# Latent attention: values of two key tiles in one place, rough pieces between the heads of a score step, 24 pieces ahead of a pair of heads

## What is computed

```python
c_q = _rmsnorm(x @ Wq_down, q_norm_w)
q = (c_q @ Wq_up).reshape(b, s, H, HD).transpose(0, 2, 1, 3)
...
c_kv = _rmsnorm(x @ Wkv_down, kv_norm_w)
k = (c_kv @ Wk_up).reshape(b, s, H, HD).transpose(0, 2, 1, 3)
...
scores = (jnp.einsum('bhqd,bhkd->bhqk', q, k) + jnp.einsum('bhqd,bhkd->bhqk', q_rope, k_rope)) * scale
attn = jax.nn.softmax(scores, axis=-1)
out = jnp.einsum('bhqk,bhkd->bhqd', attn, v)
```

## Time and profile before

| | us |
|---|---|
| median of 3 runs | 2254.46 |
| the runs | 2253.89 to 2258.62 |
| the profiled execution | 2254.67 |
| its span, from the first to the last instruction | 2252.9 |
| a pair in the middle of a sequence | 61.3 |

### The profile page before, as it was taken

One profiled execution on the slowest core, in us unless ns is written; L12 is line 12 of the kernel. 1 busy time (PEld: TensorE's weight loads), 2 busy tenths in 40 slices (PEclk: granted clock), 3 DMA queues, 4 the chain that ended last, 5 costly groups with the idle time before them and its releaser, 6 DMA issues. The chain is left out here.

```text
span 2252.9 us, 29291 instructions
## 1 busy us (share of the span) xinstructions
PE 2004.6 (89%) x8700; PEld 1245.8 (55%) x8701; DVE 1301.1 (58%) x2970; ACT 785.7 (35%) x1293; POOL 866.8 (38%) x684
## 2 busy tenths in 40 slices
PE   5899868889888799967599999999899999999987
PEld 5566635545554666646455555555565555555456
DVE  7322275777785722237466666666656666666525
ACT  1122244555555122223223333333413333433323
POOL 0344301231112044432026555556425555565632
PEclk9999969999999599988579999999999999999999
DMA  9111132331220811132331122122122222211101
GB/s 380 47 63 58 54 122 29 42 44 29 29 29 7 341 56 60 61 103 109 73 69 42 46 56 50 38 54 56 22 63 57 57 52 56 56 45 42 31 0 50
DMA packets 60569, 150.62 MB, mean 67 GB/s; under 512 B 12977, under 2 KB 18305, under 8 KB 58177
## 3 DMA queue, kind: packets, MB, share of 16 engines
q1 hardware_dynamic: 50208, 120.43, 20.4%
q0 software_dynamic: 9120, 24.92, 3.5%
q10 hardware_dynamic: 1152, 4.19, 0.5%
HBM read 68.95 MB, written 18.61 MB: 39 GB/s over the span
## 5 line engine op out<-in xcount | busy, mean ns | idle before, releaser
L1831 POOL TENSOR_TENSOR mla_PS<-mla_PS,mla_PT 128x1024 f32<-128x1024 f32 x192 | 457.7, 2384 | 222.2 <-ACT mla_PT L2110 219.6
L2253 DVE TENSOR_REDUCE mla_MXP<-PS 128x1 f32<-128x512 f32 x512 | 343.3, 689 | 241.9 <-PE PS L1910 236.6
L2110 ACT ACTIVATE mla_PT<-PS 128x1024 f32<-128x1024 f32 x256 | 262.4, 1026 | 401.9 <-PE PS L1929 399.5
L1938 PE MATMUL PS<-mla_PT,mla_CN 128*64 128x512 f32 x1024 | 275.3, 616 | 0.1
L1910 PE MATMUL PS<-mla_KH,mla_QH 113*128 113x512 f32 x512 | 216.6, 459 | 30.1 <-DMA mla_KL<-mla_SL 18.8
L521 DVE COPY moe_HT<-PS 128x512 f32<-128x512 f32 x92 | 63.6, 692 | 306.9 <-PE PS L644 301.0
L1929 PE MATMUL PS<-mla_QH,mla_KH 113*128 113x512 f32 x512 | 211.3, 413 | 1.0 <-ACT mla_QH L2097 1.0
L675 POOL DMA_INDIRECT moe_XS<-rows_in,moe_GI x96 | 93.5, 974 | 307.1 <-PE PS L630 171.7
L1929 PE MATMUL PS<-mla_QL,mla_KH 113*128 113x512 f32 x512 | 202.2, 395 | 0.0
L1929 PE MATMUL PS<-mla_QH,mla_KL 113*128 113x512 f32 x512 | 201.3, 393 | 0.0
L1910 PEld LDWEIGHTS PS<-mla_KH,mla_QH 113*128 113x128 f32 x512 | 90.7, 193 | 192.0 <-DVE mla_MXP L2253 123.5
(11 more groups left out here) (297 smaller groups left out, 3203.2 us busy)
## 6 DMA issues: line engine op xcount, KB each, us to landing
W<-in_W_dram SPq DMA_DIRECT2D x16, 2048.0 KB, 28.1
mla_QH<-mla_SH SPq DMA_DIRECT2D x64, 128.0 KB, 2.4
mla_KH<-mla_SH SPq DMA_DIRECT2D x64, 128.0 KB, 2.4
mla_QL<-mla_SL SPq DMA_DIRECT2D x64, 128.0 KB, 2.5
mla_KL<-mla_SL SPq DMA_DIRECT2D x64, 128.0 KB, 2.4
mla_KH<-mla_SH SPq DMA_DIRECT2D x64, 96.0 KB, 2.4
mla_KL<-mla_SL SPq DMA_DIRECT2D x64, 96.0 KB, 2.4
sums_Y<-rows_out SPq DMA_DIRECT2D x9, 512.0 KB, 6.1
```

The lines of the kernel that those rows point to most:

```text
L1831: pool.tensor_tensor(PS[:, :], PT[:, slot(0), :] if k == 1 else PS[:, :], PT[:, slot(k), :], ALU.add).then_inc(s_ps.handle, 1)
L1938: ins = pe.matmul(bank(6)[h * DKVL:(h + 1) * DKVL, :], CN[:, b, k, 0:DKVL], PT[:, slot(k), h * HB:(h + 1) * HB], start=(k == 0), stop=(k = ...
L2110: act.activation(PT[:, slot(k), :], banks(st_bank(s, 0), 2)[:, :], ACT.Exp, scale=MLA_SCALE).then_inc(s_p.handle, 1)
L2253: dve.tensor_reduce(MXP[:, n // NPC, c, h, t:t + 1], bank(piece_bank(n))[:, :], AX_X, ALU.max).then_inc(s_mx.handle, 1)
```

## The change

The values of step m are no longer computed in step m + 1, each in a place of its own. The table `WITH` puts those of two steps together: at step 0 those of the last two steps of the pair before, at 2, 4 and 6 those of steps 0 to 5, at 7 and 8 one each (steps 6 and 7, the end of a query block), at 10, 12 and 14 those of steps 8 to 13. Steps 1, 3, 5, 9, 11, 13 and 15 have none. `PT`'s three slots now go round (`SLOT`), and `exp_of` waits for what `in_slot_until` names. The first rough piece of a step moves between the two heads of `scores_of`, except at steps 2 and 9. In the second half of a pair the second piece stands ahead of the values. `LATE` sums to 24 instead of 22, `EARLY` to 8 instead of 10. ACT's `out_copy` of the block before moves behind the first exponential of a pair.

```diff
-    LATE, EARLY = {9: 3, 10: 3, 11: 3, 12: 3, 13: 4, 14: 3, 15: 3}, {2: 1, 3: 2, 4: 3, 5: 2, 6: 2}
+    LATE, EARLY = {9: 2, 10: 4, 11: 3, 12: 4, 13: 3, 14: 5, 15: 3}, {2: 2, 3: 1, 4: 2, 5: 1, 6: 2}
...
-    slot = lambda k: 2 if k == 0 else k % 2
+    WITH = {0: (-2, -1), 2: (0, 1), 4: (2, 3), 6: (4, 5), 7: (6,), 8: (7,), 10: (8, 9), 12: (10, 11), 14: (12, 13)}
+    SLOT = (0, 1, 2, 0, 1, 2, 0, 1, 2, 0, 1, 2, 0, 1, 2, 1)
+    in_slot_until = lambda s: max(p for p in range(-NS, s) if SLOT[p % NS] == SLOT[s])
...
                             for n, (kk, qq) in enumerate(((KH, QH), (KH, QL), (KL, QH))):
                                 ins = pe.matmul(bank(st_bank(s, h))[:, :], kk[USED, buf, h, ks], qq[USED, buf, h, qs], start=(n == 0), stop=(n == 2))
+                            if h == 0:
+                                rough_scores(*near, between)
                         ins.then_inc(s_st.handle, 1)
...
-                            scores_of(it, buf, s, first and s < 2)
+                            between = 0 if s in (2, 9) else 1
+                            scores_of(it, buf, s, first and s < 2, near, todo[:between])
...
-                            if s == 8:
-                                denominators(2 * it)
-                            rough_scores(*near, todo[:1])
-                            if s == 0 and not first:
-                                denominators(2 * it - 1)
...
+                            rough_scores(*near, todo[between:1 if s < TB else 2])
+                            if s == 8:
+                                denominators(2 * it)
+                            if s == 0 and not first:
+                                denominators(2 * it - 1)
                             if s or not first:
-                                values_of(NS * it + s - 1, 2 * it + (s - 1) // TB, (s - 1) % TB)
-                            rough_scores(*near, todo[1:2])
+                                for m in WITH.get(s, ()):
+                                    values_of(NS * it + m, 2 * it + m // TB, m % TB, m % NS)
...
-                            rough_scores(*near, todo[2:])
+                            rough_scores(*near, todo[1 if s < TB else 2:])
...
                         if last:
-                            values_of(NS * it + NS - 1, 2 * it + 1, TB - 1)
+                            for m in (NS - 2, NS - 1):
+                                values_of(NS * it + m, 2 * it + m // TB, m % TB, m % NS)
...
-                        if not free:
-                            if k == 0:
-                                act.wait_ge(s_ps.handle, s_ps.at((TB - 1) * (blk - 1) + 1))
-                                act.wait_ge(s_v.handle, s_v.at(TB * (blk - 1) + 1))
-                            else:
-                                act.wait_ge(s_v.handle, s_v.at(NS * it + s - 1))
-                                act.wait_ge(s_ps.handle, s_ps.at((TB - 1) * blk + (k - 2 if k > 2 else k - 3 + 2 * (k == 1))))
+                        p = in_slot_until(s)
+                        if p >= 0 or not free:
+                            act.wait_ge(s_v.handle, s_v.at(NS * it + p + 1))
+                            act.wait_ge(s_ps.handle, s_ps.at((TB - 1) * (2 * it + p // TB) + max(p % TB, 1)))
```

More of the change, by code:

```diff
@@ L1830, in sums @@
                                 pool.wait_ge(s_ps.handle, s_ps.at((TB - 1) * blk + k - 1))
-                            pool.tensor_tensor(PS[:, :], PT[:, slot(0), :] if k == 1 else PS[:, :], PT[:, slot(k), :], ALU.add).then_inc(s_ps.handle, 1)
+                            pool.tensor_tensor(PS[:, :], PT[:, SLOT[TB * q], :] if k == 1 else PS[:, :], PT[:, SLOT[TB * q + k], :], ALU.add).then_inc(s_ps.handle, 1)
                     def pair(it, r, buf, first, last, after=None):
@@ L1918, in max_rows, with scores_of @@
                         ins.then_inc(s_mt.handle, 1)
-                    def scores_of(it, buf, s, free):
+                    def scores_of(it, buf, s, free, near, between):
                         q, k = s // TB, s % TB
@@ L1929, in scores_of, with values_of @@
                                 ins = pe.matmul(bank(st_bank(s, h))[:, :], kk[USED, buf, h, ks], qq[USED, buf, h, qs], start=(n == 0), stop=(n == 2))
+                            if h == 0:
+                                rough_scores(*near, between)
                         ins.then_inc(s_st.handle, 1)
-                    def values_of(step, blk, k):
+                    def values_of(step, blk, k, at):
                         pe.wait_ge(s_p.handle, s_p.at(step + 1))
@@ L1937, in values_of @@
                         for h in range(2):
-                            ins = pe.matmul(bank(6)[h * DKVL:(h + 1) * DKVL, :], CN[:, b, k, 0:DKVL], PT[:, slot(k), h * HB:(h + 1) * HB],
+                            ins = pe.matmul(bank(6)[h * DKVL:(h + 1) * DKVL, :], CN[:, b, k, 0:DKVL], PT[:, SLOT[at], h * HB:(h + 1) * HB],
                                             start=(k == 0), stop=(k == TB - 1))
@@ L2102, in exp_of @@
                         act.wait_ge(s_st.handle, s_st.at(NS * it + s + 1))
-                        if not free:
-                            if k == 0:
-                                act.wait_ge(s_ps.handle, s_ps.at((TB - 1) * (blk - 1) + 1))
-                                act.wait_ge(s_v.handle, s_v.at(TB * (blk - 1) + 1))
-                            else:
-                                act.wait_ge(s_v.handle, s_v.at(NS * it + s - 1))
-                                act.wait_ge(s_ps.handle, s_ps.at((TB - 1) * blk + (k - 2 if k > 2 else k - 3 + 2 * (k == 1))))
-                        act.activation(PT[:, slot(k), :], banks(st_bank(s, 0), 2)[:, :], ACT.Exp, scale=MLA_SCALE).then_inc(s_p.handle, 1)
+                        p = in_slot_until(s)
+                        if p >= 0 or not free:
+                            act.wait_ge(s_v.handle, s_v.at(NS * it + p + 1))
+                            act.wait_ge(s_ps.handle, s_ps.at((TB - 1) * (2 * it + p // TB) + max(p % TB, 1)))
+                        act.activation(PT[:, SLOT[s], :], banks(st_bank(s, 0), 2)[:, :], ACT.Exp, scale=MLA_SCALE).then_inc(s_p.handle, 1)
                     def out_copy(blk):
@@ L2118, in pair @@
                         for s in range(NS):
-                            if s == 0 and not first:
-                                out_copy(2 * it - 1)
                             if not last:
@@ L2129, in pair @@
                                     weights_high(it + 2, r + 2)
-                            exp_of(it, s, first and s < 3)
+                            exp_of(it, s, first)
+                            if s == 0 and not first:
+                                out_copy(2 * it - 1)
                             if not last:
```

## The result

| | before | after |
|---|---|---|
| median, us | 2254.89 (8 runs) | 2269.88 (8 runs) |
| the runs, us | 2251.04 to 2258.62 | 2263.5 to 2275.38 |
| span of the profiled execution, us | 2252.9 | 2268.4 |
| a pair in the middle of a sequence, us | 61.4 | 62.3 |

The ratio is 1.0064, with a 95% interval of 1.0054 to 1.0075: 15 us, slower. The forecast was 2260, slower by 5, with a range of 2234 to 2273. The pair lengths here are distances between the joins of step 13, over six pairs (1742.1 to 2110.3 before, 1749.8 to 2123.9 after), which the moved exponential of step 0 does not disturb.

The account below looks back on a forecast made before the run. PE, busy 59.6 of a middle pair's 61.3 us, was taken as the bound. Terms summed to +0.44, taken as +0.55 a pair, +7.7 over 14 pairs; with the ends +5.4 on 2254.67 gave 2260 us, range 2234 to 2273.

Parts of the forecast that it names:

- values side by side, 7 places: Values in a middle pair go from 16 places to 9; each merging gives 0.35 us on PE: -2.45 a pair.
- `max_rows` at step 7: Join still ends with POOL's add, 4.15 us stays; PE waits 0.24 instead of 0.87 us: -0.63 a pair.
- `max_rows` at step 14: Join of step 13 asks 0.3 to 0.4 us behind the add's start and waits for its end: +1.82.
- the slow piece, from step 13 to step 14: Step 13's fourth piece cost 0.83 us, waiting for a maximum; the same wait comes behind step 14's values: 0.
- denominators at step 0: PE arrives at 3.54 us but POOL's last add lets it go at 4.14: +0.60 a pair.
- small waits of pieces: Pieces wait for bank A maxima at steps 2 to 5, +0.72, and behind `latent_out` at step 12, +0.4: +1.1.
- a price between the heads: Rival: nine pieces each followed at 0.34 instead of 0.23 us, with 0.05 wait; 1.4 a pair, 2280 us; chance 0.14.
- one of my own signs of being wrong: The forecast is wrong if distances behind pieces between the heads are mostly 0.34 us.
- The ends: Last pair about -2.4 us, last pair of the first sequence -1.2, two more pieces ahead of the first pair +1.3.
- At nothing: Two pieces more ahead of a pair are two fewer in it, put down at no cost.

Follow-up runs that it names:

- one input: The kernel after, with DVE's join of the maxima as a reduction over one SBUF input: 2240.22 us, ratio 0.9941. The same edit on the kernel before: 2256.56 us.
- half an add: The kernel after, with POOL adding only 512 of 1024 columns in adds behind a block's first, computing something else: 2242.9 us, ratio 0.9944.
- the run with the pieces of steps 3 and 5: The kernel after, with the piece of steps 3 and 5 behind the scores instead of between their heads: 2267.53 us, ratio 1.0065.
- the run with none between: The kernel after with the one-input join and all pieces behind the scores, none between the heads: 2247.64 us, ratio 0.9966.
- the runs with the tables: The kernel after with before's LATE and EARLY: 2295.12 us; with before's LATE and two early pieces in each of steps 2 to 6: 2281.72 us.

## Why the prediction came out as it did, by its own steps

The terms for a middle pair, forecast and as the traces show them:

| term | forecast | measured |
|---|---|---|
| values side by side, 7 places | -2.45 | -2.4 |
| `max_rows` at step 7 | -0.63 | -0.6 |
| `max_rows` at step 14 | +1.82 | +1.68 |
| the slow piece, from step 13 to step 14 | 0 | 0 |
| denominators at step 0 | +0.60 | +0.44 |
| small waits of pieces | +1.1 | +1.7 |
| behind the projection of step 3 | not in it | +0.2 |
| sum; the pair itself | +0.44, taken as +0.55 | +1.0; +1.0 |

**Values side by side** held: 1.87 us for two groups to the next piece, as denominators and values had shown it. **The join at step 14** held in mechanism, place and size: it asked 0.29 behind the add (forecast 0.3 to 0.4), and `max_rows` stood 3.90 behind the piece after the scores (3.89). The wait is 1.68 and not 1.82 because PE itself came later, 2.20 behind that piece and not 2.07: a small wait lies in between. The runs with one input and with half an add show that it is POOL's add and DVE's second input, not argued only. **Step 7** held to 0.02: `max_rows` stood 4.16 behind the last score matmul of step 6 (4.15), and waited 0.24. **The slow piece** kept its distance, 1.28 from the first piece behind the values to the third (1.29). **The denominators** wait 0.44 and not 0.60: step 15 has a small wait of its own, and what PE waits there it does not wait later. In the loop's other pair PE waits about as long already at the next pair's first scores, and not at the denominators.

**The small waits** are the term that was mis-sized, +1.7 for +1.1. I had counted two in bank A and one behind `latent_out`. In the later half too, pieces at steps 10 to 15 come a few hundredths before their maximum is ready. The wait itself is 0.02 or so, but the matmul behind it then comes at 0.34 and not 0.23, and that happens at seven places. My rival of a price between the heads named this mechanism, with nine places and 1.4 us; seven places came, with about 0.9. And one of my own signs of being wrong came true: of the ten pieces between the heads of a middle pair, six (steps 3, 5 and 10 to 13) have 0.34 behind them and not 0.23, so the distances there are mostly 0.34. I had held that DVE's reductions leave room, and they fall short of it by 0.02 us. That such a wait cannot be taken away one by one is what the run with the pieces of steps 3 and 5 shows; that the pieces are still better between the heads than behind them, the run with none between.

**Left out of the sum** was the projection of step 3. Before, a group of values stood right behind it, and the 0.32 from the one to the other was counted as the price of the group. Now scores stand there, and they come 0.32 and 0.33 apart instead of 0.23 (1836.08, 1836.41 and 1836.74 in this trace): 0.2 us.

**The ends** were another miss. For the pairs at the ends and the start I had written -2.3 us. The span grew by 15.5. Of that, 14 pairs at 0.97 are 13.6, and the one pair in which the clock fell is 2.8, so about -0.9 is left for the ends. The last pair was to take its merging whole. It did not: its POOL adds follow each other nearly without a gap, ACT waited for them and PE waited once 1.75 us (1.05 before) for the last of them ahead of the denominators at step 0, and 0.98 (0.72 before) ahead of `max_rows` at step 7, because the join there lay under an add again. **"At nothing"** for the two pieces was wrong in general, as the runs with the tables show, though right that nothing was to be seen of it in this sum.

So the sign, the range and the cause held, and the size fell short by 10 us, 0.4%. Of these, 5.9 us lie in the 14 pairs (+0.97 for +0.55, the small waits and the projection of step 3), 1.4 at the ends, and 2.8 in the one pair with the fallen clock, of which the prediction says nothing. Whether that last part belongs to the change or to this execution the runs do not tell.

## What to carry to other kernels

Merging work that the busiest engine does in small groups pays what the distances in the trace say, but each group that moves was also cover for someone's wait: list who is late next before adding up. In these traces a tiny instruction cost two microseconds because it read two SBUF tensors on DVE while POOL added, so look for durations that are far longer than their shape, and for short instructions that end exactly with another engine's; a reduction over one input does the same work and did not wait here. And a wait that has gone is only worth what the next chain leaves of it: 0.2 of 0.85 us in the kernel before.

## What the runs showed of the hardware that I had not expected

A maximum of two SBUF operands and a reduction over one SBUF operand with the same data take the same 0.17 us when POOL is silent; 0.29 us into a POOL add of 2.35 us the first took 2.09 and the second 0.17. A matmul of 512 columns whose start is delayed by only 0.02 us by a semaphore is followed by the next at 0.34 us instead of 0.23: the delay costs a tenth of a microsecond beyond itself. In the fourteen traces together, pieces that stood 0.25 us behind the matmul ahead were followed at 0.33 to 0.35 in 514 of 573 places, those at 0.24 in 71 of 364, and those at 0.23 in none of 852.

The granted clock fell in the middle of the steady pairs in four of the traces: after, before with the one-input join, after with the halved adds, and the merging undone with the one-input join. It went to the 1.2 GHz level for 3.4 or 6.8 us, during or within 2 us behind a wait of PE of 1.4 to 2.7 us at step 9, and the pair became 1.5 to 4.2 us longer, the longer wait included. Most waits of 1.4 us in the last of these traces were followed by no fall.
